# Mixture-of-experts decoder block on one core: in the last stage each gather also waits for the landing of the gather two places before it

## The reference

```
scores  = softmax(xt @ Wg.T)                    # 2048 tokens, 16 experts
topi    = top 4 of the experts in the best 2 of 4 groups
y[t]    = sum over the 4 chosen experts e of  scores[t,e] * W2_e(silu(W1_e xt) * W3_e xt)
z       = Ws2 (silu(Ws1 xt) * Ws3 xt)           # shared expert, twice the width
out     = x + y + z
```

## Time and profile before

| what | value |
|---|---|
| median of three runs | 1920.51 us |
| the profiled execution: its time, its span | 1920.77 us, 1919.0 us |
| PE, DVE, ACT, POOL busy, share of the span | 79%, 57%, 33%, 35% |
| last stage | about 1802 to 1919 us |
| the 64 gathers: first and last start | 1803.33 us, 1902.59 us |
| the 64 combines: first and last start | 1811.4 us, 1913.6 us |

### The profile page before, as it was taken

The page is one execution under the profiler, slowest core; times in us unless marked ns, Lnnn a source line. Parts: engine busy times, 40 slices in busy tenths (PEclk is TensorE's granted clock), DMA queues, the critical chain, the costliest instruction groups (busy, mean ns, idle before and its releaser), DMA issues. The chain is left out here.

```text
span 1919.0 us, 29165 instructions
## 1 busy us (share of the span) xinstructions
PE 1515.1 (79%) x9516; PEld 701.8 (37%) x9525; DVE 1094.0 (57%) x1809; ACT 625.1 (33%) x1103; POOL 681.2 (35%) x685
## 2 busy tenths in 40 slices
PE   1778787887157888888888847881899999999988
PEld 1334343434012222222222215340555555556443
DVE  6443444444557888888888547730354544444376
ACT  4312130303225656665666646110111111111121
POOL 3000000000445323323330021664464645676364
PEclk9989898898656898899999976995999999999999
DMA  4160708080346211211211012143666657563465
GB/s 175 49 204 26 227 0 252 0 251 1 101 105 176 53 42 39 56 40 39 56 38 19 1 48 94 61 170 131 186 177 162 164 144 176 157 203 88 118 188 182
DMA packets 183543, 211.00 MB, mean 110 GB/s; under 512 B 89968, under 2 KB 135600, under 8 KB 182960
## 3 DMA queue, kind: packets, MB, share of 16 engines
q1 hardware_dynamic: 154224, 123.73, 24.0%
q0 software_dynamic: 18592, 66.99, 11.4%
q10 hardware_dynamic: 10656, 19.40, 2.6%
HBM read 101.09 MB, written 88.87 MB: 99 GB/s over the span
## 5 line engine op out<-in xcount | busy, mean ns | idle before, releaser
L804 DVE TENSOR_REDUCE ca_mx<-ca_sc 128x1 f32<-128x512 f32 x512 | 327.6, 678 | 93.7 <-PE ca_sc L724 93.4
L77 PE MATMUL re_ab<-fx_w,re_xt 128*128 x1800 | 296.6, 315 | 52.3 <-DMA re_xt<-slot_rows 52.2
L937 ACT ACTIVATE ca_pt<-ca_st 128x512 f32<-128x512 f32 x512 | 264.7, 596 | 106.7 <-PE ca_st L736 106.7
L724 PE MATMUL ca_sc<-ca_ks,ca_qs 48*128 48x512 f16 x512 | 191.6, 428 | 54.3 <-DVE ca_mx L804 29.8
L77 PEld LDWEIGHTS re_ab<-fx_w,re_xt 128*128 128x128 f16 x1800 | 173.6, 98 | 150.7 <-issue 54.7
L736 PE MATMUL ca_st<-ca_qs,ca_ks 49*128 49x512 f16 x512 | 173.1, 402 | 40.9 <-ACT ca_pt L937 35.2
L77 PE MATMUL re_yp<-fx_w,re_ht 128*128 (+1 forms) x666 | 156.0, 379 | 0.0
L478 POOL TENSOR_TENSOR sa_yt<-sa_yf,sa_yt 128x512 f16<-128x512 f32 x16 | 18.5, 1158 | 385.4 <-ACT sa_yt L461 385.4
L1492 POOL TENSOR_TENSOR fx_w<-re_raw_w,fx_w 128x272 f16<-128x272 f32 x224 | 154.2, 725 | 1.7
L749 PE MATMUL ca_pv<-ca_pt,ca_va 128*32 128x512 f32 x1024 | 150.0, 650 | 1.0 <-DVE ca_turned L817 0.5
L77 PE MATMUL sh_ab<-fx_xn,sh_pair 128*128 (+3 forms) x576 | 129.7, 388 | 3.8 <-PEq L1420 3.3
(11 more groups left out here) (236 smaller groups left out, 2437.0 us busy)
## 6 DMA issues: line engine op xcount, KB each, us to landing
re_raw_w<-in_we POOLq DMA_DIRECT2D x56, 544.0 KB, 4.7
slot_rows<-sa_zeros SPq DMA_DIRECT2D x12, 1792.0 KB, 16.1
slot_outs<-re_ys ACTq DMA_DIRECT2D x74, 256.0 KB, 2.0
sa_scratch<-sa_qk SPq DMA_DIRECT2D x16, 512.0 KB, 4.8
ca_scratch<-ca_qk SPq DMA_DIRECT2D x64, 128.0 KB, 1.8
sa_qs<-sa_scratch SPq DMA_DIRECT2D x12, 512.0 KB, 7.1
sa_ks<-sa_scratch SPq DMA_DIRECT2D x12, 512.0 KB, 7.0
ca_qs<-ca_scratch SPq DMA_DIRECT2D x48, 128.0 KB, 3.7
```

The costliest lines, as they stand in the source:

```text
L77: last = nc.tensor.matmul(out, lhs(a, c), rhs(b, c), start=(c == 0 and n == 0), stop=(c == chunks - 1 and n == len(PRODUCTS) - 1))
L724: nc.tensor.matmul(sc[:, m % RING, :], qs[rows, c % SLOTS, pair, qt * P:(qt + 1) * P], ks[rows, c % SLOTS, pair, :], start=True, stop=True ...
L804: nc.vector.reduce_max(mx[:, qd // 4, qd % 4, 2 * a + jj:2 * a + jj + 1], sc[:, m % RING, :], AX.X).then_inc(maxed, 1)
L937: nc.scalar.activation(pt[:, (4 * qd + k) % 8, :], st[:, m % RING, :], ACT.Exp, scale=SCALE).then_inc(exp_done, 1)
```

## The change

In `combine_and_share`, in POOL's loop over the gathers, a second wait is put between the wait for the place in the ring and the gather:

```
             for m, (t, k) in enumerate(fetches):
                 if m >= RING:
                     pool.wait_ge(used, m - RING + 1)
+                if m >= ABREAST:
+                    pool.wait_ge(fetched[(m - ABREAST) % RING], 16 * ((m - ABREAST) // RING + 1))
                 nc.gpsimd.indirect_dma_start(
                     out=yg[:, m % RING, :], out_offset=None, in_=slot_outs,
```

## The result

| | before | after |
|---|---|---|
| median of the runs measured together | 1919.08 us | 1944.24 us (1941.51 to 1947.55) |
| ratio, 95% interval | | 1.0132 (1.0105 to 1.0159) |
| profiled execution: time, span | 1920.77, 1919.0 us | 1941.51, 1939.8 us |
| first gather's start | 1803.33 us | 1794.65 us |
| first gather to the end of the span | 115.7 us | 145.1 us |

The kernel became 25 us slower; 13.5 us were forecast, and the time lies 2 us outside the range. The two profiles reach the last stage at different times although nothing ahead of it differs. Over the fourteen profiles of this study that start lies anywhere between 1790 and 1806 us, so I compare the last stage by itself: it grew by 29.4 us.

A forecast was written before the change was run, and what follows sets the result against it. DVE's combines set the gathers' pace before. With P at 3.7 us combine 63 comes 9.0 us late, plus 4.5 for three stores: 13.5 us on 1920.77 gives 1934.3, stated as 1934.0 for the median; range 1926 to 1942 us.

The forecast's parts named there:

- the path: Last stage: late gathers delay DVE's combines 23, 39 and 55 ahead of the adds, and PE and the end equally.
- the ring lead: Gathers' lead over DVE's combines, today up to eight; claimed to be used up and never refilled.
- The term for the clock: PE's lower clock after a wait: if longer idle deepens it, each of three restarts costs up to 1 us more.
- start to last packet: First part of P: from a gather's start to the last of its 16 semaphore packets, taken as 3.15 us.
- the second part of P: From a gather's last packet to the start of the one two places on, taken from the scatters as 0.55 us.
- P: Period from a gather's start to that of the one two places on, landing in between: 3.7 us.
- the waiting instruction itself I cost at nothing: The 62 added waits on POOL were taken to cost nothing in themselves, as in the routing stage's scatters.
- the price of a store: Lateness of gathers from each 1 MB output store: 1.5 us taken, between 0 and 2.1 us; three ahead of combine 63.
- the contention with DVE: POOL against DVE: a waiting DVE was said to disturb less; less contention would shorten the combines by 0.6 us at most.
- Large loss: Rival: P near 3.9 us and 2.1 us for each store, time about 1942 us; chance 0.16.
- Small loss: Rival: P about 3.4 us and stores that cost nothing, time 1923.5 us; chance 0.08.
- not slower: Rival: P under 3.1 us as in the scatters, no combine late, time 1920.5 us; chance 0.06.

The follow-up runs named there:

- x2_met: The changed kernel with the landing wait moved from two to eight gathers back, so that it is always met; ratio to the kernel before 0.9989.
- x1_swap: The changed kernel with its two waits in the other order, landing first and place in the ring second; ratio to the kernel before 1.0118.

## Why the prediction was wrong

**Right: the path.** The gathers became the bound, the lateness of DVE's combines ahead of a round's first add went into PE's idle time, and the ring lead was never refilled. PE's idle time grew by 25.7 us (34.5 - 8.8), nearly the lateness of combine 55 (26.3); the rest of the stage's 29.4 is combine 63, which waits for its own landing behind the third store. The term for the clock, up to 1 us for each of three restarts, is borne out: the 18 matmuls from 1845.71 took 6.01 us at a mean granted clock of 0.67 and those from 1881.77 took 6.74 at 0.59, against 5.75 and 5.74 at 0.70 before (all four are mixtures of the 1.2 and the 2.4 GHz level). It did not set the end, for DVE waited for gathers again. That nothing else on POOL matters and the last store's end is as before held too.

**Right: start to last packet.** Forecast 3.15 us; measured by packets, nearly all lie between 2.9 and 3.3. The Trainium skill's fit (DMA: Bandwidth & Descriptors, Anatomy of one DMA — SWDGE (gpsimd) path) gives 2.6 us for 256 KB; the trace has 2.9 at the least, before the follower's start is counted.

**Wrong: the second part of P.** The 0.55 us for "last packet to the next start" was read off the scatters of the routing stage. Those have one wait each; the gathers from the ninth on have two. Their follower starts 1.1 us after the last packet, so P was 4.1 and not 3.7. For the six gathers with one wait (2 to 7) the term was right: the first periods are 3.65 and 3.44 us. The sentence "the waiting instruction itself I cost at nothing" holds where the wait is met (x2_met) and fails where it blocks.

Over the 28 periods from gather 7 to 63 the difference is 28 x 0.46 = 12.9 us, with 4.16 as the mean outside the stores.

**Wrong: the price of a store.** The stores cost 7.4 to 7.6 us for three, where 4.5 were taken ("with two in flight there is less queued than with three") and 6.3 was the upper bound. That bound was misread. The 544 packets up to 1856.3 are not all of gathers; the same view lists the packets by queue:

```profile
q0 software_dynamic: 2716, 8.91, 59.4%
q1 hardware_dynamic: 485, 0.99, 5.0%
```

The 34 gathers to number 33 need 34 x 80 = 2720 packets of q0, the gathers' queue, so the last of them had not come yet; three of the 544 are the store's own. By queue, gather 33's 16th small packet starts at 1856.8, 5.9 us after the gather's start and 2.5 more than its neighbours, not 5.4 and 2.1.

Together, combine 63 is late by 13.5 + 12.9 + 2.9 = 29.3 us on the clock of the profile before, against 29.4 measured. The medians differ by 25.2 us, 4 less; with a stage that is itself 3.5 us shorter in the second profile of the kernel before, the sum can't be held to better than that.

**The other cover.** I had named the contention with DVE ("a DVE that waits disturbs less") as a reason for a short period. The swap shows the contrary for a follower that starts at once: gather and combine are released by the same landing, so in the odd series they meet every time. With the waits in the other order the loss is nearly the same (ratio 1.0118 against 1.0132), by the other mechanism.

**The rivals.** Large loss was nearest, but for another reason than the one given (a loaded landing of 3.35 us), and its 1942 was short. Its 0.16 was too little, and the range, which leaned on 4.0 us as the largest P, too narrow. Small loss and not slower are out: no period under 3.4 us is in the trace after. DVE's first wait for a landing comes at combine 8, not 14, and PE's wait in the first round grew to 14.95 us, not to about 10.

## What to carry to other kernels

When a wait is added to an instruction that already has one, look in the trace for how a wait in that form is released, not only for how long the awaited thing takes: here 0.5 us on each of 28 periods in series, in both parities at once. A bound on transfers in flight costs (landing + release) / number in flight; compare it with the pace of the consumer in its densest stretch, and count other transfers on the same engines as lateness that stays. And if one experiment that removes a suspected cost changes nothing, see whether the parts of the interval moved: another cost may have been waiting behind it.

## What the runs showed of the hardware

- A gather's part on POOL takes 0.95 us alone. What a combine of 0.75 us on DVE adds depends on which of the two starts first. Over the fourteen profiles, a gather that starts while a single combine still has 0.2 to 0.3 us to run is longer by some 0.13 us, with 0.4 to 0.5 us left by 0.3 to 0.4 us, with 0.5 to 0.7 us left by 0.4 to 0.5 us: about the rest of the combine, less 0.15 us. A gather that starts at the combine's end, or together with it (0.70 us or more left), takes 0.95 to 0.96 us; where the combine starts behind the gather, the rows vary from 0.95 to 1.3. The Trainium skill (SBUF — State Buffer, SBUF: two separate sides) says that a DVE instruction with two inputs in SBUF contends with a GpSimd operation that reads SBUF, and infers (section Who interferes with whom) that descriptor generation is not held up by it. The combine has two such inputs and the gather reads its 128 indices from SBUF, so the lengthening of 0.4 to 0.5 us in x1_swap agrees with the first; no run separates the reading of indices from the rest.
- A wait for a landing that stands on the gather itself releases it 0.6 us after the start of the last packet (0.62 us for the scatters of the routing stage); one in an instruction of its own ahead of the gather, 1.1 us after it. That instruction's record is 17 ns, whether it blocks (changed kernel) or not (x2_met).
- One store of 1 MB beside two gathers in flight makes one period longer in each parity: by 2.3 to 2.65 us in the odd series of the changed kernel, by 0.7 to 2.2 us in the even one.
- Code that is equal up to there reaches the last stage anywhere between 1790 and 1806 us, over fourteen profiles.
